# Four retention blocks and a mixture of experts on one core: biases and group statistics as split float32r products, idle products at the start, a new order on all engines

## The reference

```python
h = xn
for l in range(4):                       # Wkqv, Wm1, ... are layer l's
    k, q, v = split(h @ Wkqv, 3)
    r = tril(q @ k.T / sqrt(128)) / (1 + sqrt(row))
    r = r / clip(abs(r.sum(-1)), 1, None)
    a, gate = split(r @ v @ Wm1 + bm1, 2)
    m = (a * silu(gate)) @ Wm2 + bm2
    y = groupnorm(m) * gn_g + gn_b + h   # one mean, one variance per sequence
    f = gelu(y @ Wf1 + bf1) @ Wf2 + bf2
    h = layernorm(f + y) * ln_g + ln_b
# experts: the two largest of 8 gate logits per token, softmax over them
cw = weights of the two chosen experts, 0 for the other six
out = x + h + sum_e cw[e] * (xn @ We[e].T + be[e])
```

## Time and profile before

| | us |
|---|---|
| median of 3 runs | 467.02 (466.91 to 467.07) |
| the profiled execution | 466.61 |
| its span, first to last instruction | 464.5 |
| TensorE busy | 437.6 (94%) |
| VectorE busy | 384.8 (83%) |
| ScalarE busy | 237.9 (51%) |
| GpSimd busy | 228.2 (49%) |

### The profile page before, as it was taken

One profiled execution on the slowest core, in us unless ns is written; L12 is line 12 of the kernel. 1 busy time (PEld: TensorE's weight loads), 2 busy tenths in 40 slices (PEclk: granted clock), 3 DMA queues, 4 the chain that ended last, 5 costly groups with the idle time before them and its releaser, 6 DMA issues.

```text
span 464.5 us, 8143 instructions
## 1 busy us (share of the span) xinstructions
PE 437.6 (94%) x2366; PEld 332.1 (71%) x2366; DVE 384.8 (83%) x1335; ACT 237.9 (51%) x447; POOL 228.2 (49%) x246
## 2 busy tenths in 40 slices
PE   3898999999999999999999999999999999999870
PEld 2887887777777877777677777777777777775540
DVE  5779889878888887888878887888878888888875
ACT  2123584655545555555555555565555655564432
POOL 3653113554555455344355443444536444578792
PEclk9999989999999999999999999999999999999995
DMA  8900000000000000000000000000000000001102
GB/s 235 248 1 0 3 1 0 2 0 2 1 2 0 2 1 0 2 0 2 1 1 0 3 1 0 3 0 2 0 1 2 1 1 1 1 23 37 33 23 68
DMA packets 13498, 8.21 MB, mean 18 GB/s; under 512 B 608, under 2 KB 13456, under 8 KB 13456
## 3 DMA queue, kind: packets, MB, share of 16 engines
q1 hardware_dynamic: 13376, 7.68, 5.8%
q10 hardware_dynamic: 80, 0.02, 0.0%
HBM read 5.60 MB, written 2.10 MB: 17 GB/s over the span
## 4 chain that ended last, share of the span: by engine, by line
PE 83%; DVE 10%; issue 3%; POOL 2%; DMA 1%; ACT 0%; ACTq 0%; POOLq 0%; DVEq 0%
PE bank L262 9%; PE bank L263 8%; PE bank L266 8%; PE bank L435 6%; PE bank L431 6%; PE bank L341 6%; PE pair L347 6%; PE bank L324 6%; PE bank L397 5%; PE bank L331 5%; PE pair L349 4%; PE pair L270 3%; PE bank L373 3%; PE bank L270 3%; PE bank L283 2%
## 5 line engine op out<-in xcount | busy, mean ns | idle before, releaser
L1192 POOL TENSOR_TENSOR sum_four<-prod 128x512 f32<-128x512 f32 x32 | 50.2, 1568 | 61.3 <-issue 58.7
L1186 POOL TENSOR_TENSOR y_part<-y,y_part 128x512 fp32r<-128x512 f32 x32 | 40.7, 1272 | 75.4 <-ACT y_part L659 75.4
L681 ACT ACTIVATE va<-bank,ln_off,ln_r 128x128 f32<-128x128 f32 x128 | 48.3, 464 | 14.4 <-DVE ln_off L996 14.4
L635 ACT ACTIVATE a_in<-bank,params 128x512 f32<-128x512 f32 x32 | 22.0, 687 | 59.5 <-PE bank L266 59.5
L347 PEld LDWEIGHTS pair<-va,scores 128*128 128x128 f32 x256 | 41.5, 192 | 14.5 <-issue 13.9
L347 PE MATMUL pair<-va,scores 128*128 128x129 f32 x256 | 49.9, 276 | 0.0
L652 ACT ACTIVATE hg<-vt,gn_c,g_prev 128x512 f32<-128x512 f32 x32 | 26.1, 815 | 42.2 <-DVE gn_c L960 42.2
L1004 DVE TENSOR_TENSOR prod<-bank,route 128x512 f32<-128x512 f32 x64 | 43.9, 686 | 0.1
L1167 POOL TENSOR_TENSOR ln_r<-ln_v,minus_half 128x4 f32<-128x4 f32 x32 | 32.7, 1022 | 21.4 <-DVE ln_v L988 21.1
L262 PE MATMUL bank<-ot,b_w 128*128 128x512 f32 x64 | 39.6, 619 | 1.9 <-DVE ot L907 1.9
L1162 POOL TENSOR_TENSOR gn_r<-gn_v,minus_half 128x1 f32<-128x1 f32 x32 | 17.6, 549 | 46.7 <-DVE gn_v L948 46.6
(11 more groups left out here) (159 smaller groups left out, 1181.0 us busy)
## 6 DMA issues: line engine op xcount, KB each, us to landing
x_in<-in_L_attn_x_dram SPq DMA_DIRECT2D x8, 256.0 KB, 5.3
out_dram<-x_in SPq DMA_DIRECT2D x8, 256.0 KB, 2.3
wf<-in_L_attn_Wf_dram SPq DMA_DIRECT2D x2, 512.0 KB, 6.5
kqv<-in_L_attn_Wkqv_dram SPq DMA_DIRECT2D x1, 576.0 KB, 6.5
expert_rows<-in_L_ffn_We_dram SPq DMA_DIRECT2D x1, 512.0 KB, 7.6
wm<-in_L_attn_Wm_dram SPq DMA_DIRECT2D x1, 384.0 KB, 6.8
wm<-in_L_attn_Wm_dram SPq DMA_DIRECT2D x1, 256.0 KB, 4.8
expert_b<-in_L_ffn_be_dram SPq DMA_DIRECT2D x16, 4.0 KB
```

Source lines behind the costliest of these rows:

```text
L681: last = act.activation(va[:, n % NB, c, 0:D], Z_BANK[:, c * P:(c + 1) * P], ACT.Identity, bias=ln_off[:, i, c:c + 1], scale=ln_r[:, i, c: ...
L1186: pool.tensor_tensor(y_part[:, 1, :], y[:, n % 2, :], y_part[:, 0, :].bitcast(F32), ALU.subtract).then_inc(y_rest, 1)
L1192: pool.tensor_tensor(sum_four[:, :, :], prod[:, 0:4, :], prod[:, 4:8, :], ALU.add).then_inc(four_set, 1)
```

## The change

Four things, beside new numbers for the PSUM banks.

1. The two group-norm products are done in float32r. The column of means becomes two columns, a rounded part and its rest, and the matrix of 1/128 is held as `mean_r` (1/128 is exact in it). One matmul of 2 columns takes the place of a float32 product of 1 column; VectorE makes the parts with two more small instructions for each (four an item) and adds the two result columns in the instructions that read them.
2. The biases' product is done in float32r with 128 rows: `spread_route` copies the route four times side by side, 8 transposes instead of 2 turn it, and rows 64 to 127 hold its rest; `bias_w` holds the biases and, in blocks 1 and 3, their rest. So all four combinations of parts are summed in one matmul.
3. `keep_busy` issues products whose result nobody reads (12, 4, 1 and 3 of them) between the first instructions of TensorE.
4. The order of every engine's slots is new. `expert_rows` and `expert_b` live in space of `gelu` and `zt`.

```diff
+        mean_r = sb("mean_r", P, P, dtype=F32R)
+        route_four = prod[:, :, :].rearrange("p k (i r) -> p k i r", r=CE)
+        route_t = sb("route_t", P, NB, P, dtype=F32R)
+        bias_w = sb("bias_w", P, C, D, dtype=F32R)
...
-                pe.wait_ge(gn_means, n + 1)
-                vacated(n, (past_set, -4), (gn_veps, 1))
-                pe.matmul(GN_BANK[:, 0:1], mean_of[:, :], gn_m[:, n % 2:n % 2 + 1], start=True, stop=True).then_inc(gn_mean, 1)
+                pe.wait_ge(gn_m_rest, n + 1)
+                vacated(n, (past_set, -4), (prod_a, 3))
+                pe.matmul(GN_BANK[:, 0:2], mean_r[:, :], gn_m2[:, n % 2, :], start=True, stop=True).then_inc(gn_mean, 1)
...
-                pe.matmul(BIAS_BANK[:, :], route_t[of, b, :], expert_b[of, :, :].rearrange("p c d -> p (c d)"),
+                pe.matmul(BIAS_BANK[:, :], route_t[:, k, :], bias_w[:, :, :].rearrange("p c d -> p (c d)"),
...
+            def keep_busy(count):
+                for _ in range(count):
+                    pe.matmul(banks[0][:, 0:P], mean_of[:, :], mean_of[:, :], start=True, stop=True)
+            pe.wait_ge(means_set, 1)
+            keep_busy(12)
             pe.wait_ge(consts_in, 16)
             pe.wait_ge(kqv0_in, 16)
-            turn_kqv(0, banks[3])
-            fold(0, banks[2])
+            turn_kqv(0, banks[2])
+            keep_busy(4)
+            fold(0, banks[3])
+            turn_in(0, banks[5])
...
-                step(group_mean, n - 8)
+                step(group_mean, n - 10)
...
+            def spread_route():
+                act.wait_ge(route_set, 1)
+                act.copy(route_four, route[:, :, :].rearrange("p (k c) e -> p k (c e)", k=NB).unsqueeze(2).to_broadcast((P, NB, P // CE, CE))).then_inc(route_spread, 1)
+            def round_route(h, bank):
+                act.wait_ge(route_turned, h + 1)
+                act.copy(route_t[:, h * BATCH:(h + 1) * BATCH, :].rearrange("p b t -> p (b t)"), bank[:, :]).then_inc(route_rounded, 1)
...
+            def rest_of_route(h, bank):
+                dve.wait_ge(route_rounded, h + 1)
+                of = route_t[P // 2:, h * BATCH:(h + 1) * BATCH, :].rearrange("p b t -> p (b t)")
+                dve.tensor_tensor(of, bank[P // 2:, :], of.bitcast(F32), ALU.subtract).then_inc(route_t_set, 1)
...
+                dve.tensor_scalar(gn_m2[:, n % 2, 0:1], gn_mv[:, n % 2, 0:1], params[:, B2, l:l + 1], None, ALU.add).then_inc(gn_m_rounded, 1)
                 dve.tensor_scalar(cols(gn_m, n), gn_mv[:, n % 2, 0:1], params[:, B2, l:l + 1], None, ALU.add).then_inc(gn_means, 1)
+                dve.wait_ge(gn_m_rounded, n + 1)
+                dve.wait_ge(gn_means, n + 1)
+                dve.tensor_scalar(gn_m2[:, n % 2, 1:2], gn_m2[:, n % 2, 0:1].bitcast(F32), -1.0, cols(gn_m, n),
+                                  ALU.mult, ALU.add).then_inc(gn_m_rest, 1)
...
+            def split_biases():
+                pool.wait_ge(be_in, 16 * (P // E))
+                pool.tensor_copy(bias_w[:, :, :], expert_b[:, :, :]).then_inc(bias_rounded, 1)
+                pool.wait_ge(bias_rounded, 1)
+                for i, part in enumerate((1, 3)):
+                    of = slice(part * CE, (part + 1) * CE)
+                    pool.tensor_tensor(bias_w[of, :, :], expert_b[of, :, :], bias_w[of, :, :].bitcast(F32),
+                                       ALU.subtract).then_inc(bias_w_set, 1)
+                    pool.wait_ge(bias_w_set, i + 1)
```

More of the change, by code:

```diff
@@ L571, in slot @@
[L571 to L575 removed]
+                if n == 12:
+                    pe.wait_ge(o_set, 5)
+                    turn_route(0, banks[0])
+                if n == 9:
+                    pe.wait_ge(past_set, 4)
+                    turn_in(6, banks[2])
+                if n == 8:
+                    pe.wait_ge(past_set, 3)
+                    turn_kqv(1, banks[2])
@@ L576, in _ @@
+                if n == 6:
+                    pe.wait_ge(xt_set, 2)
+                    turn_in(3, banks[5])
+                if n == 7:
+                    turn_in(5, banks[6])
+                step(ask_experts_b, n - 12)
+            for n in range(ITEMS + 14):
                 slot(n)
@@ L763, in _ @@
-            for n in range(ITEMS + 12):
+                if n == 17:
+                    round_f1(1)
+                if n == 16:
+                    round_route(1, banks[1])
+                if n == 14:
+                    set_logits(1, banks[4], (3, 4))
+                step(set_v, n - 17)
+                step(set_gelu_b, n - 15)
+                if n == 0:
+                    set_xt(1, banks[5])
+                if n == 14:
+                    set_kqv_t(2, banks[5])
+                step(set_gt, n - 10)
@@ L764, in _ @@
+                if n == 14:
+                    set_logits(3, banks[3], (7,))
+                if n == 12:
+                    set_xt(6, banks[2])
+            for n in range(ITEMS + 17):
                 slot(n)
@@ new lines, in slot @@
+                if (n - 15) % C == 0:
+                    step(add_biases, n - 15)
+                step(weigh_b, n - 15)
+                step(set_y, n - 13)
+                step(norm_stats, n - 15)
+                step(past_first, n - 8)
+                step(rest_of_ot, n - 11)
+                step(norm_aggr, n - 15)
+                if n == 1:
+                    read_in(2)
+                if n == 4:
+                    normalise_in(2)
+                if n == 14:
+                    set_route()
@@ new lines, in slot @@
+                step(denominators, n - 10)
+                step(group_means, n - 12)
+                step(divide_first, n - 10)
+                if n == 11:
+                    rest_of_experts(0, banks[5])
+                if n == 2:
+                    read_in(3)
+                if n == 6:
+                    read_in(5)
+                step(divide_second, n - 10)
+                step(group_dev, n - 12)
+                if n == 8:
+                    rest_of_b(0, banks[3])
+                step(gate, n - 11)
@@ new lines, in slot @@
+                if n == 31:
+                    rest_of_b(3, banks[1])
+                if n == 9:
+                    derive()
+                if n == 14:
+                    rest_of_route(1, banks[1])
+                step(set_z, n - 14)
+                step(group_scale, n - 12)
+                if n == 14:
+                    rest_of_b(2, banks[5])
+                step(group_coef, n - 12)
+                if n == 0:
+                    read_in(1)
+                if n == 11:
+                    rest_of_b(1, banks[6])
@@ L1288, in _ @@
+                if n == 4:
+                    in_factor(4)
+                if n == 25:
+                    rest_of_f1(2)
+                step(group_factor, n - 14)
+                if n == 16:
+                    shift_x(1)
+            for n in range(ITEMS + 19):
                 slot(n)
```

613 lines of the change are left out of this document (280 added, 333 removed).

## The result

The changed kernel takes 461.05 us (median; 459.13 to 462.88), the kernel before beside it 466.97 (466.53 to 467.07). The ratio is 0.9875, with a 95% interval of 0.9834 to 0.9915. So it is faster, but by 5.9 us and not by 17: the prediction of 450.0 and its range of 444.5 to 457.0 missed. The profiled execution took 461.07 us with a span of 459.3. In one experiment (`gn_plain_in_after`) the profiled execution took 892 us, with TensorE's products at half speed throughout; it is left out, and that kernel's stages are read from a sibling (`lnv_gn_plain`).

What follows compares the result with a forecast made beforehand. TensorE was taken to bound the middle of the kernel, not its two ends. 466.6 - 5.7 - 7.1 - 3.3 - 1.0 = 449.5, plus 0.4 for the median, rounded to 450; range 444.5 to 457.

Steps and rivals of the forecast that it cites:

- The two product terms: TensorE's middle: cheaper group-norm products save 5.7 us, cheaper biases' products 7.1 us.
- The group-norm term: Mean's and variance's products on TensorE: 0.11 saved twice an item, 0.22, in some 26 items, 5.7 us.
- the biases' product: TensorE, slots with a bias: from 1.24 us to one record of 0.23, seven times 1.01, 7.1 us saved.
- the rival in which the load is paid: Biases' product on TensorE: its weight load is not hidden, 453 us in all; chance 0.04.
- What VectorE gets: Four small VectorE instructions an item, 0.7 to 0.8 us, fit with 0.5 us to spare and cost nothing.
- the answer for the variance: Middle slots: the variance's product on TensorE was to have its operand about 0.5 us ahead.
- The slower rival: Added VectorE instructions held up while GpSimd works, in 26 items: about 498 us, slower than before; chance 0.04.
- The row that I set against it (L953): A one-column VectorE instruction took 0.20 us with GpSimd busy; cited against added instructions being held up.
- The end: Last 30 us: a feed product's wait goes, three VectorE-bound slots carry 0.8 us more each; net 1.0 us off.
- The wait of the earlier trace: Near the end, a feed product's wait of 1.61 us for `prod` was to go, the two no longer sharing a bank.
- The start: First 80 us: idle products raise the clock and early products run in half the time; 3.3 us off.
- the start gives nothing: First slots fill later and the clock falls twice: 3.3 us lost again, 453 to 457 us; chance 0.11.
- VectorE the bound: VectorE takes over as the bound, slot as long as before, group-norm saving gone: 455 to 456 us; chance 0.12.

Runs made afterwards that it cites:

- gn_plain_in_after: The changed kernel with plain float32 group-norm products, without their four VectorE instructions, `ln_v` left on VectorE: 458.68 us, ratio 0.9818.
- lnv_gn_plain: The changed kernel with `ln_v` on GpSimd and plain float32 group-norm products, without their four VectorE instructions: 458.94 us, ratio 0.9825.
- lnv_on_gpsimd: The changed kernel with `ln_v` (variance plus epsilon) computed on GpSimd instead of VectorE: 455.62 us, ratio 0.9756.
- lnv_split_middle: The changed kernel with `ln_v` on GpSimd and split group-norm products for items 4 to 27 alone, plain elsewhere: 453.41 us, ratio 0.9707.
- middle_wide: The changed kernel with `ln_v` on GpSimd, split group-norm products for items 4 to 27 alone, and logit products 128 columns wide: 452.6 us, ratio 0.9684.
- wide_logits: The changed kernel with each logit product 128 columns wide instead of 8: 459.96 us, ratio 0.9828.

## Why the prediction was wrong, step by step

**The two product terms were right as prices.** The group-norm term (0.22 an item) measured 0.21, the biases' product 0.23 with no load paid, so the 7.1 us came and the rival in which the load is paid did not. But of the 24 x 0.22 = 5.3 us that the group norm should bring between the 4th and the 28th item, 307.78 - 299.02 - 6 x 1.01 = 2.7 arrived: 0.1 us a slot went to the late gn_p.

Two readings beside these terms were off, without moving the sum. The 0.38 us that the old biases' product cost over its two passes was not the wait of its 32-row load alone. The full-height load behind it (in the kernel before) waited as long:

```profile
230.42 0.19 PEld L262 LDWEIGHTS bank<-expert_w,xn 128*128 128x128 f32 x1 [0.76 <-issue]
```

L435 starts at 228.34, L455 at 229.37 and the L262 behind it at 230.43: 1.03 and 1.06 us for two pairs of passes of 0.86. So about half of the 0.38 lay on each side of L455; why is not shown, and the change altered rows and type together. The other is the rule of the Trainium skill (TensorE: Matmul & The Clock Gate, Part 3, The mechanism). The matmul that runs ahead of the 32-row load uses all 128 rows, those 32 among them, so by the rule that load should not get ahead either, and the trace agrees. The same section also lets a load go ahead into the background weight buffer, so the full-height loads that overlap do not speak against the section as a whole.

**The step that failed is "What VectorE gets".** It counted what the change adds (0.7 to 0.8 us, at nothing) and took what was there at its old price. The four added instructions take 0.19 to 0.27 us each and are not held up, as the one-column row said. Three old ones that now read two result columns instead of one (`gn_d`, `gn_b`, `gn_v`) went from 209, 207 and 157 ns to 275, 273 and 217, another 0.19 us an item that the prediction did not count; the groups of the first, before and after:

```profile
L938 DVE TENSOR_SCALAR gn_d<-bank,gn_m 128x1 f32<-128x1 f32 x32 | 6.7, 209 | 0.1
```

```profile
L981 DVE TENSOR_SCALAR gn_d<-gn_m,bank 128x1 f32<-128x1 f32 x32 | 8.8, 275 | 1.9 <-PE bank L410 1.8
```

The larger part came from the order, which moved `ln_v`, four columns wide, beside GpSimd's 512-column work, and its mean grew by 0.73 us. VectorE had hardly any idle time left in a slot of 12.36 us (96.8 us of 100 busy), where 0.5 us had been counted on, and the answer for the variance, "0.5 us ahead", came late. Shown by `lnv_on_gpsimd`: 2.4 us back in the middle and 0.9 at the end.

**The slower rival had the right mechanism on the wrong instructions.** It let the added ones be held up and asked 498 us. In the order of before that is what happened: 507.7, through `ln_mr`. The row that I set against it (L953) only spoke for one-column instructions; L996, four wide and at 1.19, stood in the same group, and four-column instructions like it (`ln_v`, `ln_mr`) were the ones to follow through the whole of the new order.

**The end: 1.0 us off predicted, 4.3 us on measured** (70.5 to 74.8, 5.3 over the predicted 69.5). The wait of the earlier trace rows went, as said. But the term charged VectorE for three slots of 0.8 and set larger gains against it. With plain products in the last four items, so without the four instructions, the end is 3.1 us shorter (73.9 to 70.8), and with `ln_v` moved 0.9. Of the 3.1, 1.7 lie ahead of the last mean product. The other 1.4 lie behind it, and most of that may be the clock: with the split it fell there (L441 takes 1.92 us in `lnv_on_gpsimd`, 1.02 in `lnv_split_middle`), and in `middle_wide`, where it fell without the split, that stretch is 1.0 longer. What is left, 70.8 against the 69.5 that before would have with its last biases' product at the new price, is 1.3 us that no run takes apart; that it lies in the new order is not shown. Gains were booked where VectorE, by the prediction's own words, was the bound.

**The start: 3.3 us off predicted, 0.7 on measured** (86.22 - 85.50 less the 1.01 + 0.44 of the products up to there). The product price and the idle products came, also the first attending product 3.2 us earlier. Then the clock fell twice, as the rival "the start gives nothing" had it. From after to `wide_logits`, where it held, the 4th mean product moves by 1.8 us; from there to `middle_wide`, where VectorE is relieved too, by 1.6. That 1.6 is the plain products of the first four items and not `ln_v`: `lnv_on_gpsimd`, whose clock held as well, has 83.93, no earlier than the 83.66 of `wide_logits`. The sum, 82.09, is 0.6 from the predicted 81.5. These are single profiles of each kernel, so the split between the two is good to about half a us. The idle products alone change no total that the runs can tell.

Of the rivals, three came at once in part (VectorE the bound, the start, the hold-up). I had given each a chance as if the others stayed away, and cut the range at 457.

## What to carry to other kernels

When an order is changed, price every short instruction again by what will run beside it on GpSimd, not only the new ones: a four-column VectorE instruction went from 0.2 to 1.2 us, and moving one or two such to GpSimd was worth up to 5 us here (3.3 of them followed in the middle and the end) and 41 us there. A change that trades TensorE's time for VectorE's belongs only in the stretch where TensorE is the bound; it can be left off for the first and last items. A full PE row can hide a late operand: look for weight loads whose idle time ends with another engine.

## What was not expected of the hardware

- Which VectorE instructions are held up beside GpSimd's 256- and 512-column ones: over whole programs 128x4 instructions on SBUF operands took 942 (`tensor_scalar`, `ln_v`) and 1053 ns (`tensor_tensor`, `ln_mr`) in the orders that put them there, 212 and 188 in the order of before. The 128x1 ones stayed at 157 to 275 ns. The width alone does not decide: the three 128x4 instructions of `den`, two that read PSUM and a reciprocal, stayed at 0.12 to 0.18 us inside GpSimd's work. On GpSimd the 128x4 work of `ln_v` and `ln_mr` took 231 and 200 ns.
- A single float32r product of two columns, its load made ahead, costs 0.11 us in all (0.03 between its neighbours' starts, 0.08 in the later start of the second product behind it); with its operand just late it costs 0.1 more, with no idle time in PE's row.
- 24 logit products took 2.67 us to the next start with 8 columns and 2.75 with 128, so the wider form costs next to nothing and seems to keep the clock.
- In the first comparison the changed kernel's executions spread by 0.8% (0.971 mean clock at 462.88 us, 0.984 at 459.13), those of before by 0.1% (by up to 0.5% in the later comparisons): the clock's falls at the two ends are not the same in each execution.
